# One layer of attention, experts and Mamba on one core: q and k made channel by channel, stacked by SBUF-to-SBUF transfers, scores of two heads in row halves

## The reference, cut to what matters

```python
def _attn(x, ln_w, ln_b, conv_w, attn_w, proj_w, n_head):
    h = _layernorm(x, ln_w, ln_b)
    h = depthwise_causal_conv(h, conv_w)            # three taps
    q, k, v = jnp.split(h @ attn_w, 3, axis=-1)     # 16 heads of 8 channels
    q = q * cos + _rotate_half(q) * sin
    k = k * cos + _rotate_half(k) * sin
    scores = jnp.einsum('bqhd,bkhd->bhqk', q, k) / jnp.sqrt(D)
    scores = jnp.where(causal, scores, -1e30)
    p = jax.nn.softmax(scores, axis=-1)
    return jnp.einsum('bhqk,bkhd->bqhd', p, v).reshape(B, T, C) @ proj_w
def _moe(x, ...):          # 4 experts, 128 -> 2 x 512 -> 128, one chosen by argmax
    for e in range(4):
        gate_raw, value = jnp.split(h @ expert_wv[e], 2, axis=-1)
        y = gate_raw * sigmoid(gate_raw) * value @ expert_proj[e]
        out = out + jnp.where((expert_idx == e)[..., None], y, 0.0)
x = x + 0.5 * block(layernorm(x)); x = x + mamba_mlp(layernorm(x)); x = x + 0.5 * block(layernorm(x))
```

## Time and profile before

| what | value |
|---|---|
| median of 3 runs | 2296.11 us (2294.92 to 2296.81) |
| span of the profiled execution | 2293.9 us |
| PE busy | 1976.4 us, 86% |
| PE weight loads busy | 1038.1 us, 45% |
| DVE busy | 1528.3 us, 67% |
| ACT busy | 1054.4 us, 46% |
| POOL busy | 280.5 us, 12% |

### The profile page before, as it was taken

One profiled execution on the slowest core, in us unless ns is written; L12 is line 12 of the kernel. 1 busy time (PEld: TensorE's weight loads), 2 busy tenths in 40 slices (PEclk: granted clock), 3 DMA queues, 4 the chain that ended last, 5 costly groups with the idle time before them and its releaser, 6 DMA issues. The chain is left out here.

```text
span 2293.9 us, 35596 instructions
## 1 busy us (share of the span) xinstructions
PE 1976.4 (86%) x11712; PEld 1038.1 (45%) x11824; DVE 1528.3 (67%) x3811; ACT 1054.4 (46%) x1650; POOL 280.5 (12%) x305
## 2 busy tenths in 40 slices
PE   4788898897969899889796988898879789989978
PEld 2344444453434444444443444454444445444443
DVE  6477487584848758667584876857757585784844
ACT  3534535453543544545353453554535355445451
POOL 1011202101001220210101021021010103112100
PEclk8988998998989999999898999999989899999998
DMA  2000000000000000000000000000000000000000
GB/s 91 1 1 6 1 5 1 1 1 6 1 7 1 6 1 5 2 1 1 5 1 7 5 2 1 6 1 1 2 5 2 5 1 1 1 1 1 1 6 5
DMA packets 11935, 11.25 MB, mean 5 GB/s; under 512 B 864, under 2 KB 10464, under 8 KB 11744
## 3 DMA queue, kind: packets, MB, share of 16 engines
q1 hardware_dynamic: 11744, 8.84, 1.3%
HBM read 6.74 MB, written 2.10 MB: 4 GB/s over the span
## 5 line engine op out<-in xcount | busy, mean ns | idle before, releaser
L560 PE MATMUL wring<-scratch,wv 128*128 128x512 f32 x1024 | 548.6, 644 | 21.9 <-DVE scratch L1101 19.0
L1037 DVE TENSOR_REDUCE mx<-aring 128x1 f32<-128x512 f32 (+3 forms) x704 | 429.4, 638 | 203.7 <-PE aring L494 200.2
L748 ACT ACTIVATE prob_mem<-aring 128x512 f32<-128x512 f32 x640 | 363.2, 597 | 274.5 <-PE aring L509 272.1
L774 ACT ACTIVATE scratch<-wring 128x512 f32<-128x512 f32 x256 | 152.6, 596 | 517.8 <-PE wring L560 516.3
L507 PE MATMUL aring<-stq,stkT 128*128 128x384 bf16 (+3 forms) x975 | 251.5, 312 | 66.2 <-DVE mx L1037 35.3
L492 PE MATMUL aring<-stkT,stq 128*128 128x384 bf16 (+3 forms) x961 | 251.0, 306 | 33.6 <-DVE mx L1037 24.7
L560 PEld LDWEIGHTS wring<-scratch,wv 128*128 128x128 f32 x1024 | 188.0, 204 | 187.2 <-issue 122.3
L535 PE MATMUL acc<-scratch,ep 128*128 128x512 f32 x512 | 262.8, 595 | 0.5 <-DVE scratch L1115 0.5
L698 ACT ACTIVATE stq<-aring 64x1024 bf16<-64x1024 bf16 x192 | 195.2, 1017 | 92.0 <-PE aring L419 90.5
L509 PE MATMUL aring<-neg_queries,identb 128*128 128x128 bf16 x1024 | 192.9, 225 | 23.3 <-ACT stq L698 19.7
L1109 DVE SCALAR_TENSOR_TENSOR scratch<-scratch,wring 128x512 f32<-128x512 f32 x256 | 174.4, 681 | 52.8 <-ACT scratch L774 51.5
(11 more groups left out here) (206 smaller groups left out, 2592.1 us busy)
## 6 DMA issues: line engine op xcount, KB each, us to landing
x<-in_x SPq DMA_DIRECT2D x8, 256.0 KB, 2.8
wv<-in_wv SPq DMA_DIRECT2D x1, 2048.0 KB, 10.7
out_x<-x SPq DMA_DIRECT2D x8, 256.0 KB, 2.2
w<-in_w SPq DMA_DIRECT2D x2, 256.0 KB, 4.8
W_in<-in_W_in SPq DMA_DIRECT2D x1, 322.0 KB, 12.1
attn_w<-in_attn_w SPq DMA_DIRECT2D x1, 192.0 KB, 2.8
W_out<-in_W_out SPq DMA_DIRECT2D x1, 128.0 KB, 3.9
ident<-in_consts SPq DMA_DIRECT2D x1, 64.0 KB, 1.9
```

The costliest lines, as they stand in the source:

```text
L560: last = pe.matmul(ring[:], wv[:, e, o:o + P], hm[e % 2][:], start=True, stop=True)
L748: act.activation(probs[x % EXPS], ring[:], ACT.Exp, scale=float(HD) ** -0.5).then_inc(a_freed[t % SLOTS], 1)
L1037: dve.tensor_reduce(dst, src_ap, AX_X, ALU.max).then_inc(a_freed[t % SLOTS], 1)
```

## The change

1. **q and k channel by channel.** `qk` step 0 makes q and step 1 makes k with channels in the partitions, each in a plain and in a half-rotated copy (two products of 512 columns, one bank each), the weights put into that order on the host. `v` is a step of its own. The rotation is then three full-width operations on VectorE per side, and the split into pieces six contiguous copies and subtractions of 128x512.
2. **Stacks filled by transfers.** SyncE copies the pieces from SBUF to SBUF into `stk[0]` (queries) and `stk[1]` (keys): 24 transfers of 64 KB per attention. The eight `qkT` steps with their transposes and copies are gone. The first `max` fill waits for all 24.
3. **Row halves.** One head sits in rows 0 to 63 of the stacks, its partner in rows 64 to 127. The score product of each reads 48 rows (50 with the maximum), into a bank of its own. The masks come first, as full-height products of 128 or 2x128 columns.
4. **Two-bank slots.** A slot of `aring` is two banks, `SLOTS` is 2 for both rings. A group has 5 `max` and 5 `exp` fills of up to 1024 columns, read by one or two reductions, or one exponential. `proj` now uses a slot.
5. **The shift.** The maximum goes in two bf16 pieces; TensorE transposes only those (8 rows), ScalarE copies them out, and SyncE brings them into the query stack in two transfers per group. `shift` of a group stands right behind its fifth `max`; two `max` fills of the next group stand between it and the first `exp`.
6. **Order.** `TURNS` is replaced by `merged`, which spreads the steps of both lanes over each stretch by shares in a table. SyncE follows the same schedule.

The diff, cut to its core:

```diff
-NPROD = 6
-EXPS = 10
+HALF = 64
+TILES = 5
+PRODUCTS = (((0, 1), (0, 2)), ((2, 3), (0, 4)), ((4,), (1, 0)))
+Q_ROWS = ((0, 1, 2), (3, 5), (4,))
+K_ROWS = ((2, 3, 4), (1, 5), (0,))
+STACK_DMAS = 24
...
 def attention_steps():
...
+    LAG = 1
+    at = []
     for g in range(GROUPS):
+        for k in range(TILES):
+            at += [(TILES * g + k, ("max", g, k)), (TILES * (g + 1) + LAG + k + 0.5, ("exp", g, k))]
+        at.append((TILES * g + TILES - 0.9, ("shift", g)))
+        if g + 1 < GROUPS:
+            at.append((TILES * (g + 2) + LAG + 2.6, ("back", g)))
+    steps = [("stats",), ("norm",), ("hT",), ("qk", 0), ("qk", 1), ("v",), ("high",), ("mid",), ("low",)]
+    steps += [step for _, step in sorted(at)]
...
-SLOTS = 3
+SLOTS = 2
...
-TURNS = (
...
+def merged(phases):
...
+            left = [k for k in range(2) if at[k] < len(shares[k])]
+            k = min(left, key=lambda k: (done[k] + shares[k][at[k]] / 2) / total[k])
...
+        order = merged([(sa, se + sm), (sa, se + sm), (sa, se), ([] if last else sa, se)])
...
-        aring = [pb(f"aring{i}", [P, 512]) for i in range(SLOTS)]
+        aring = [pb(f"aring{i}", [P, 2, 512]) for i in range(SLOTS)]
...
+                def stack(side, piece, product):
+
+                    for a in range(2):
+                        row = HALF * a + HD * product
+                        sp.dma_start(stk[side][row:row + HD, :, :],
+                                     piece[side][HALF * a:HALF * a + HALF, :]).then_inc(s["a_stacked"], 16)
...
+                        sp.wait_ge(s["a_shiftT"], n * GROUPS + g + 1)
+                        for piece in range(SHIFTS):
+                            sp.dma_start(stk[0][MROW + piece:P:HALF, 2 * g:2 * g + 2, :],
+                                         shiftT[GROUP * piece:GROUP * (piece + 1), :]).then_inc(s["a_shifted"], 16)
...
+                        for r in range(2):
+                            w0 = (2 * side + r) * P
+                            last = pe.matmul(ring[:, r, :], attn_w[:, w0:w0 + P], cT[:], start=True, stop=True)
...
+                        if (g, k) == (0, 0):
+                            pe.wait_ge(s["a_stacked"], (n + 1) * STACK_DMAS * 16)
+                        masked(ring, neg_keys, max_blocks(k), lambda c, w: c + w - P)
+                        for q, j, c, w in max_blocks(k):
+                            for a in range(2):
+                                rows = slice(HALF * a, HALF * a + MROW)
+                                last = pe.matmul(ring[:, a, c:c + w], stk[0][rows, 2 * g + q, j * P:(j + 1) * P],
+                                                 stk[1][rows, 2 * g + q, 0:w], start=False, stop=True, skip_group_check=True)
...
-                        for q, a, kb, c, w in blocks(k // 2, k % 2):
-                            hp = 2 * g + q
-                            pe.matmul(ring[:, c:c + w], stkT[:, hp, kb * P:(kb + 1) * P], stq[a][:, hp, T - w:T],
-                                      start=True, stop=False)
-                            last = pe.matmul(ring[:, c:c + P], identb[:], neg_queries[:], start=False, stop=True)
...
+                            act.wait_ge(s["a_rope"], 2 * n + side + 1)
+                            copy(high[side][:], rqk[side]).then_inc(s["a_high"], 1)
...
+                        act.activation(prob_mem[:, k], ring[:], ACT.Exp, scale=float(HD) ** -0.5).then_inc(freed, 1)
...
+                        dve.tensor_tensor(rc[side], ring[:, 0, :], cosT[:], ALU.mult)
+                        dve.tensor_tensor(rs[side], ring[:, 1, :], sinT[:], ALU.mult).then_inc(freed, 1)
                         a_used(dve, n, task)
+                        dve.tensor_tensor(rqk[side], rc[side], rs[side], ALU.add).then_inc(s["a_rope"], 1)
```

431 lines of the change are left out of this document (214 added, 217 removed).

## The result

The changed kernel takes 2671.68 us (median of 4 runs, 2665.24 to 2674.11), the kernel before 2295.52 us beside it: a ratio of 1.1636, 95% interval 1.1619 to 1.1653. The prediction was 2252 us with a range of 2150 to 2370; the time lies 300 us above its upper end.

The account below looks back on a forecast made before the run. PE was taken as nearest its limit but not full. PE -24, new waits +118 and gains -138 us made -44: 2293.9 to 2250, plus 2.2 from span to median, 2252 us; range 2150 to 2370.

Parts of the forecast that it names:

- What bounds the kernel: Profile reading: PE is nearest its limit but not full, busy 144.3 of 160.4 us with Mamba, 104.5 of 121.8 without.
- The third row shows where the second kind leaks: With experts alone, PE is idle 18.4 us from 1195 to 1251; spreading the experts fills it: -91 us.
- (b): Chain from statistics to qk has fewer expert products ahead: +21 us beside experts alone, +8 with Mamba.
- Beside Mamba, the -40 us: DVE bounds the first third of the Mamba stage, so lighter reductions save 5 us, 8 times: -40 us.
- PE, scores: Score products in two row halves at once save 8.6 of some 17.3 us per attention.
- PE, changes of shape: Going between full-height masks and row halves costs 0.24 us per fill, 40 fills: +9.6 us per attention.
- DVE and ACT: Fewer or lighter operations save 11 and 17 us per attention, counting only where those engines hold PE up.
- (a): First score fill waits for the stack transfers: +48 us beside experts alone, +16 with Mamba.
- The rival of slow transfers: Stack transfers slower than the loads, 0.85 us each instead of 0.46: 2357 us, slower; chance 0.22.
- (c): shift follows its fifth max with nothing between in some groups: +81 us, against -56 for the old shift's wait.
- The transfers of the shift: 0.9 + 1.9 us, behind two max fills and at least two expert products (3.9 us), so hidden.
- Two slots: Two slots instead of three cost the experts at most a late weight load, 0.06 us a chunk: +1 us.

Follow-up runs that it names:

- e5_before_merged: The kernel before, with its table of turns replaced by the changed kernel's even deal, shares scaled to its own steps: 2561.26 us, ratio 1.1157.
- e10_new_table: The changed kernel's instructions in a hand-worked order of their own, with shift behind two max fills of the next group: 2310.08 us, ratio 1.0071.
- e13_full_height: e10_new_table with score products reading all 128 rows instead of one half, shift left out, scores not right: 2290.35 us, ratio 0.9983.
- e14_full_height_ok: e10_new_table with correct full-height score products, by a zero half in each query tile and two more transfers per attention: 2303.07 us, ratio 1.0038.
- e16_after_full_height: The changed kernel in its own even deal, with only the score products at full height (zero half in query tiles): 2662.61 us, ratio 1.1604.
- E1: Not a run: the kind of stretch in which an attention runs beside experts and Mamba, eight of them.
- E2: Not a run: the kind of stretch in which an attention runs beside the experts alone, seven of them.
- e9_old_order_late: The changed kernel in the order of the kernel before, with the score fills 5 to 7 steps later: 2806.13 us, ratio 1.2228.

## Why the prediction was wrong

- **What bounds the kernel: the step that failed.** "The third row shows where the second kind leaks", and the even deal fills the leak: -91 us. The idle 18 us of PE in the earlier trace rows, third row, were read as a loss that spreading the experts would take back. What the even deal takes away ahead of the scores, where a chain of single steps then runs with little beside it, was priced only for the new transfers and with 29 us in (b). The old kernel with the even deal lost 266 us (e5_before_merged), 15 to 17 in each stretch with experts alone, where -13 was taken, and 17 to 21 in each with Mamba. From -91 to +266 are 357 us, of the 420 between prediction and measurement. The two figures are of different sets of instructions, so this is a size and not a sum. The change of order was the largest part of the change, and it was the one part that got no rival.
- **Beside Mamba, the -40 us.** "Beside Mamba, DVE is the bound for the first third" brought nothing either: in e10_new_table DVE is busy for 101.5 us in such a stretch instead of 110.6, and the stretch takes 163 us instead of 160.
- **PE, scores: right.** Halves at once, 0.21 us for two products. The Trainium skill ("TensorE: Matmul & The Clock Gate", Part 3) gives 3.07 times for four row tiles, from which the prediction estimated that 2.6 of 8.6 us would stay unsaved. The rows show none unsaved for two tiles, so here the trace is better than that figure.
- **PE, changes of shape: right**, 0.21 us per fill where 0.24 was taken. Their sum with the columns was foreseen as nearly nothing, and e13_full_height, e14_full_height_ok and e16_after_full_height fit that: 7 to 20 us in favour of full height, over all attentions.
- **DVE and ACT: right in size** (9.8 and 16.3 us per attention), and worth little: with them, in an order of its own (e10_new_table), the kernel is still no faster than before.
- **New waits, (a): mis-sized.** The prediction had 0.46 us a start, 18 transfers in a row and 1.9 us behind the last, 13.2 us in all and 6.9 idle. It is 0.66, 24 in a row (the q side's are still being started when the k side's are ready) and 6.9, which gives 22.8 us from first start to release and 14.1 idle, and 10 to 12 beside E1 where 2 were taken. The rival of slow transfers had the right mechanism at 0.85 us each, where the measured mean is 22.8 / 24 = 0.95, but it kept 18 in a row and was priced as the only thing to go wrong. In all 184 us instead of 64, and 23.0 in the first attention, which the prediction left out: it took the attention that runs alone as 8 us shorter, and it was 8 longer (121.2 us instead of 113.0 from its statistics to the next).
- **(b): the wait behind the statistics.** PE's waits for the normalized input (L1018), besides the first attention, come to 15 us in 7 attentions, where 29 in 15 were taken.
- **(c): the shift.** All 64 shifts waited, 2.5 us on average, not two or three of four: 158.8 us against 81. Beside E2 it is 7 us per attention where 6.6 were taken. The miss is beside Mamba, 12.6 us instead of 4.4 and up to 6.3 at once, since the reduction stands behind Mamba's work on VectorE; the prediction had counted the reduction but not the queue ahead of it. But both (a) and (c) were waits that the order left open: e10_new_table has the same transfers and the same shift instructions, in another order, and 23 and 40 us.
- **The transfers of the shift: right**, hidden in the measured kernel (1.3 us), not in e9_old_order_late (97).
- **Two slots: nearly right.** PE's waits in front of gate and value products for the readers of their slots (L1135 and L1141, before L1109) rose from 2.8 to 12.3 us. In front of score fills, those for reductions and exponentials fell from 67 to 10 us, and are 39 in e10_new_table. So the slots are not where the time went.
- **The clock was not in the sum.** It fell from 0.932 to 0.854. PE did fewer instructions and was busy for 62 us more; with the same instructions, e5_before_merged was busy for 94 us more than the kernel before, at 0.902. A long idle time of PE costs itself and then the slower restart, as in the rows at 1095.18; in the windows from 500 on, the clock fell behind fills with short waits between them.

What stays open is the last 8 to 15 us between the two sets of instructions. The profile of e10_new_table is 12.0 us longer than that of the kernel before. Of this the start is 5.7 (the ones rows are filled for 3.47 us twice in front of the first statistics), the first attention, which has nothing beside it and waits 23.2 us for its stacks, 2.2, and against 26 more beside Mamba stand 21 less beside the experts. Why the stretches with Mamba are longer with lighter engines isn't settled; in e13_full_height they are still 9 us longer together than in the kernel before. With the whole computation at full height (e14_full_height_ok) the difference is 1 to 9 us. No version with the whole computation ran faster than the kernel before.

## What to carry to other kernels

When a change replaces a hand-set order by a rule, price that part first and by itself: put the rule on the old instructions. Idle time that one part of an order shows may be what another part gains by. A lighter engine and a hidden transfer are worth only what the order lets through, and a table of waits doesn't add up, since 54 us taken from one row came back in others. Count the changes of shape before splitting an array product to save columns: next to a mask of another shape, 0.21 us of columns saved went into 0.21 us of changes.

## What the runs showed of the hardware

- A transfer of 64 KB from SBUF to SBUF, 64 rows of 1 KB into 8 partitions, is started every 0.66 us, not 0.46 as the loads of the earlier trace rows, and 24 of them take 22.8 us, some 69 GB/s, with 75 to 78 in the middle. With half of them started from another queue it was 24.0 us.
- Two products in the upper and the lower half of the array take the time of one, and each change between full height and halves costs 0.10 to 0.11 us.
- PE's granted clock fell to 0.50 behind a run of score fills in halves, in which PE was busy for 2.40 of 4 us, and not behind the same fills at full height (2.92 and 3.07 of 4 us), in all seven attentions of that kind. Over the whole kernel the means are 0.902 and 0.943. What the clock looks at, the runs don't say.
